# Retention projects v once and sums in four column tiles; RWKV mixes on VectorE; the order of the instructions chosen anew

## The reference

```python
xk = x * time_mix_k + shifted * (1.0 - time_mix_k)     # xv, xr alike
k = jnp.einsum('bsd,ed->bse', xk, Wk)                  # v from xv, r = sigmoid from xr
# per channel, a scan over the tokens: out = (e1*aa + e2*v) / (e1*bb + e2)
out = jnp.einsum('bsd,ed->bse', r * wkv, Wo)
```

```python
q = _rotate(split_heads(x @ Wq.T), cos, sin)           # k alike; v without rotation
retention = jnp.einsum('bhsd,bhtd->bhst', q, k) * SCALING * decay   # gamma_h ** (s - t)
out = jnp.einsum('bhst,bhtd->bhsd', retention, v)
out = (out - mean) * rsqrt(var + EPS) * gn_w + gn_b    # over the 8 of a head
return silu(x @ Wg.T) * out @ Wo.T
```

## Time and profile before

| | us |
|---|---|
| runs, median (lowest to highest of 3) | 724.55 (722.36 to 731.54) |
| the profiled execution, its own time | 730.31 |
| its span | 728.4 |
| PE busy | 606.1 (83%) |
| VectorE busy | 386.8 (53%) |
| ScalarE busy | 344.1 (47%) |
| GpSimd busy | 399.4 (55%) |
| PE weight loads busy | 513.3 (70%) |

### The profile page before, as it was taken

How to read it: one execution, slowest core, us unless ns; L and a number is a source line. 1 busy time by engine, 2 the same in 40 slices (tenths; PEclk the granted TensorE clock), 3 DMA queues, 4 the chain that set the end, 5 groups by cost and what they waited for, 6 DMA issues and landing times.

```text
span 728.4 us, 13112 instructions
## 1 busy us (share of the span) xinstructions
PE 606.1 (83%) x4180; PEld 513.3 (70%) x4180; DVE 386.8 (53%) x1056; ACT 344.1 (47%) x667; POOL 399.4 (55%) x400
## 2 busy tenths in 40 slices
PE   3398998999598886888789988999678989996891
PEld 2388977678576875878778878656644659886881
DVE  6513416797679753533162206797777985500005
ACT  2355556755367534653366567314233124653450
POOL 2556756674457645655556666632205764566662
PEclk9999999999699989997999999999969999999996
DMA  8345213112311223221142213100211111211314
GB/s 335 125 135 199 41 38 102 40 38 59 95 34 30 59 49 99 73 45 33 41 105 67 45 52 96 40 19 12 81 29 23 30 29 29 66 43 44 91 45 145
DMA packets 45121, 50.21 MB, mean 69 GB/s; under 512 B 14456, under 2 KB 36344, under 8 KB 45056
## 3 DMA queue, kind: packets, MB, share of 16 engines
q0 software_dynamic: 11776, 24.14, 13.5%
q1 hardware_dynamic: 31904, 24.44, 10.6%
q10 hardware_dynamic: 1376, 0.79, 0.4%
HBM read 32.04 MB, written 17.29 MB: 68 GB/s over the span
## 4 chain that ended last, share of the span: by engine, by line
PE 63%; DVE 10%; DMA 9%; issue 8%; ACT 5%; POOL 4%; ACTq 1%; POOLq 0%; DVEq 0%
PE bank L621 18%; PE bank L601 14%; PE bank L608 10%; DMA xs<-tokens_in,idx_in 6%; PE pair L709 5%; PE pair L741 3%; PE bank L582 2%; POOL xs L1101 2%; PE pair L545 2%; PE pair L525 2%; DMA tokens_out<-ys,idx_out 2%; POOL tokens_out L1113 1%; ACT w_up L840 1%; ACT hT L861 1%; ACT ys L908 1%
## 5 line engine op out<-in xcount | busy, mean ns | idle before, releaser
L1113 POOL DMA_INDIRECT tokens_out<-ys,idx_out x184 | 195.1, 1060 | 158.4 <-ACT ys L908 80.5
L1101 POOL DMA_INDIRECT xs<-tokens_in,idx_in x184 | 193.7, 1053 | 147.1 <-DVE owner L1261 36.6
L621 PE MATMUL bank<-w,hT 128*128 x1288 | 184.5, 288 | 22.7 <-ACT ys L908 10.4
L621 PEld LDWEIGHTS bank<-w,hT 128*128 128x128 f32 x1288 | 166.6, 199 | 41.1 <-issue 39.9
L601 PE MATMUL bank<-xT_kept,w_up 128*128 128x128 f32 x1104 | 163.2, 297 | 17.6 <-ACT gate L858 6.9
L601 PEld LDWEIGHTS bank<-xT_kept,w_up 128*128 128x128 f32 x1104 | 149.2, 209 | 31.8 <-issue 17.8
L840 ACT ACTIVATE w_up<-w 128x728 f32 (+1 forms) x184 | 128.9, 718 | 47.1 <-PE bank L608 17.3
L1281 DVE TENSOR_TENSOR hT<-gate,bank 128x384 f32<-128x384 f32 x92 | 50.5, 549 | 121.8 <-PE bank L601 60.8
L608 PE MATMUL bank<-xT_kept,w_up 128*128 128x128 f32 x736 | 101.6, 286 | 10.0 <-ACT hT L861 7.3
L608 PEld LDWEIGHTS bank<-xT_kept,w_up 128*128 128x128 f32 x736 | 92.4, 197 | 20.0 <-issue 11.9
L908 ACT ACTIVATE ys<-bank 128x256 f32<-128x256 f32 x96 | 35.9, 374 | 103.0 <-PE bank L621 52.6
(11 more groups left out here) (169 smaller groups left out, 639.6 us busy)
## 6 DMA issues: line engine op xcount, KB each, us to landing
yg<-tokens_out SPq DMA_DIRECT2D x60, 128.0 KB, 3.0
w<-in_w SPq DMA_DIRECT2D x8, 536.0 KB, 8.3
w<-in_w SPq DMA_DIRECT2D x8, 512.0 KB, 5.3
xs<-tokens_in,idx_in POOLq DMA_INDIRECT x184, 2.8
tokens_out<-ys,idx_out POOLq DMA_INDIRECT x184
tokens_in<-xn SPq DMA_DIRECT2D x8, 256.0 KB, 7.1
tokens_in<-xn SPq DMA_DIRECT2D x8, 254.0 KB, 2.5
sq<-in_square SPq DMA_DIRECT2D x1, 768.0 KB, 13.2
```

The lines of the kernel that those rows point to most:

```text
L621: last = mm(y, hT[0:n_f, n % 2, c * P:(c + 1) * P], w_of(k, e, WD[k] + c * P, P, n_f), start=(c == 0), stop=(k == 0 and c == CH[k] - 1))
L1101: pool.indirect_dma_start(xs[:, j % RING, :], None, xn_dram[KIND[f]][b], tile_rows(idx_in, b, j), engine_sem=described)\
L1113: pool.indirect_dma_start(ys_dram[b], tile_rows(idx_out, b, j), ys[:, j % RING, :], None, engine_sem=described)\
```

## The change

- **Retention, v.** v is projected once per batch (2 matmuls), its rows scaled by ScalarE into `zT`, stored to a new tensor in memory (`values0`, `values1`), and loaded eight times by SP (`values(b)`), each load giving all rows of a head its value j; 4 buffers of 1024 columns (`v_own`). VectorE multiplies k by such a buffer. The 8 rounds' products lie in 5 buffers, scanned in place; the order in VectorE's stream becomes scan n, key value n+1, query n.
- **Retention, sums.** After rounds 4 and 8, four matmuls with 32 output columns each (`tile_position=(0, 32*c)`) write the four quarters of the partitions. The weights of the mean are not there any more: v's weights are centred once on VectorE (`centred_values`). The accumulator is the batch's own PSUM pair. The rows of v, g, the norm's weights and Wo are in an order of 8 by 16.
- **RWKV.** `rwkv_weights` goes. VectorE makes the difference of x and shifted x and three blends (`rwkv_mixed`, new program steps before `rwkv_exponents`), and PE needs one matmul for each projection and half.
- **Others.** SP loads and stores all of the last results. `sq` is loaded in three parts. `TURNS` is new for every engine.

```diff
...
+QUAD = 32
+NQ = P // QUAD
+ROUNDS = DH // NQ
+J_AT = [n % NQ * ROUNDS + n // NQ for n in range(DH)]
+NVB = 4
+NMB = NQ + 1
...
     "pe":
-        "d a b3 e b9 e a2 e a2 d e a d a c d c e a2 c2 a d c a e a c d a c a2 c d a d e c a2 c d a4 d a d a c a e a3 d "
...
+        "d b e b11 e a2 e a e d a2 c d a c e a3 c d a c a c2 d c a4 c d c d c e a5 e d2 a d2 a2 c a3 d c a d a c a c a "
...
-        "a d a c a b c2 b c3 b c5 a6 b4 c b2 c a2 c a4 c b6 a4 b4 a2 b2 a3 d e d a b3 d b d e4",
+        "b a2 c a c2 b c5 b c3 a6 b5 c2 b d e a3 c a2 f a c b6 a4 f5 g f4 b4 a2 g9 b2 a2 d a2 d2 b4 d e4",
...
+            def values(b):
+                yield
+                sp.wait_ge(RE_ACT[b].sem, RE_ACT[b].done(0, "v1"))
+                sp.dma_start(v_dram[b], zT[:, b, :]).then_inc(st_v[b], 16)
+                by_head = v_dram[b].rearrange("(h j) t -> h j t", j=DH)
+                for n, j in enumerate(J_AT):
+                    yield
+                    if n == 0:
+                        sp.wait_ge(st_v[b], 16)
+                        if b == 0:
+                            sp.wait_ge(RS_PE.sem, RS_PE.done(0, f"rope{2 * NH - 1}"))
+                    if n >= NVB:
+                        sp.wait_ge(RE_DVE[b].sem, RE_DVE[b].done(0, f"kv{n - NVB}"))
+                    elif b:
+                        sp.wait_ge(RE_DVE[b - 1].sem, RE_DVE[b - 1].done(0, f"kv{DH - NVB + n}"))
+                    sp.dma_start(v_own[:, n % NVB, :], by_head[:, j, :].unsqueeze(1).to_broadcast([H, DH, S]))\
+                        .then_inc(ld_v[n % NVB], 16)
+
...
             def rwkv(b):
-                def project(name, i, j, to):
-                    mm(to[:], rw_w[:, 2 * j, :], xT_of(b, i * HALF, HALF), start=True, stop=False)
-                    yield
-                    mm(to[:], rw_w[:, 2 * j + 1, :], xnT[:, b, i * HALF:(i + 1) * HALF], start=False, stop=True)\
-                        .then_inc(RW_PE[b].sem, 1)
-
+                def project(i, j, mixed, to):
+                    mm(to[:], sq[:, M_MIX + j * P:M_MIX + (j + 1) * P], mixed[:, i * HALF:(i + 1) * HALF],
+                       start=True, stop=True).then_inc(RW_PE[b].sem, 1)
+
...
-                for j in range(DH):
-                    if j + 1 < DH:
-                        for i in range(NH):
-                            yield
-                            project(i, ret[:, T_V + (j + 1) * P:T_V + (j + 2) * P], i, (RE_DVE, f"kv{j + 1}"))
+                    if i == 0 and b == 0:
+                        after(RS_COPY, 0, "gate")
+                    project(i, ret[:, T_G:T_G + P], i, (RE_ACT, f"gate{i}"))
+                for r in range(ROUNDS):
                     for i in range(NH):
                         yield
-                        if j == 0 and i == 0:
-                            after(RT_DVE[1 - b], SUB[(3, 5)[b]], "out")
-                        after(RE_DVE[b], 0, f"m{j}")
-                        mm(bank[CB[1 - b] + i][:], ret[:, T_OUT + j * P:T_OUT + (j + 1) * P],
-                           r_m[:, j % 2, i * HALF:(i + 1) * HALF], start=(j == 0), stop=(j == DH - 1)).then_inc(RE_PE[b].sem, 1)
+                        if r == 0 and i == 0:
+                            after(RS_POOL, 0, "var")
+                            after(RS_BACK, 0, "back")
+                        after(RE_DVE[b], 0, f"m{r * NQ + NQ - 1}")
+                        to = take(CB[b] + i, RE_ACT[b], 0, f"sq{i}") if r == 0 else bank[CB[b] + i]
+                        for c in range(NQ):
+                            last = mm(to[c * QUAD:(c + 1) * QUAD, :], ret[:, T_OUT + r * QUAD:T_OUT + (r + 1) * QUAD],
+                                      r_m[:, (r * NQ + c) % NMB, i * HALF:(i + 1) * HALF], start=(r == 0),
+                                      stop=(r == ROUNDS - 1), tile_position=(0, c * QUAD))
+                        last.then_inc(RE_PE[b].sem, 1)
...
-                            after(RE_PE[b - 1], 0, "x1")
+                        act.wait_ge(ld_ret, 16 * 3)
+                    after(RE_PE[b], 0, f"v{i}")
+                    run(zT[:, b, parts[i]], bank[CB[b] + i][:], ACT.Copy, RE_ACT[b], scale=scale[:, 0:1])
...
+            def rwkv_mixed(b):
+                def step(ins):
+                    ins.then_inc(RW_MIX[b].sem, 1)
+
+                def blend(out, part, c):
+                    step(V.scalar_tensor_tensor(out[:, part], rw_t[:, part], colv[:, MIX + c:MIX + c + 1], xnT[:, b, part],
+                                                ALU.mult, ALU.add))
+
+                xk, xv, xr = rw_bb[:, 1:1 + S], rw_aa[:, 1:1 + S], zT[:, b, :]
+                for i in range(NH):
+                    part = slice(i * HALF, (i + 1) * HALF)
+                    yield
+                    after(NM_ACT[b], 1, f"xnT{i}")
+                    if i == 0:
+                        after(SETUP, 0, "sel")
+                        if b:
+                            after(RW_DVE[b - 1], 0, "num")
+                    step(V.tensor_tensor(rw_t[:, part], xT_of(b, i * HALF, HALF), xnT[:, b, part], ALU.subtract))
+                    after(RW_MIX[b], 0, f"d{i}")
+                    blend(xk, part, 0)
+                yield
+                blend(xv, slice(0, S), 1)
+                yield
+                blend(xr, slice(0, S), 2)
+
...
-                for j in range(DH):
-                    m = r_m[:, j % 2, :]
-                    yield
-                    after(RE_PE[b], 0, f"v{j}_{NH - 1}")
-                    done(f"S{j - 1}" if j else "k1")
-                    step(V.tensor_tensor(r_kv, k, pair[b], ALU.mult))
-                    yield
-                    done(f"kv{j}")
-                    step(V.tensor_tensor_scan(r_S, gamma[:, 0:1].to_broadcast([P, S]), r_kv, 0.0, ALU.mult, ALU.add))
-                    yield
-                    done(f"S{j}")
-                    if j >= 2:
-                        after(RE_PE[b], 0, f"o{j - 2}_{NH - 1}")
-                    step(V.tensor_tensor(m, q, r_S, ALU.mult))
+
+                def key_value(n):
+                    if n == 0:
+                        done("k1")
+                    if n >= NMB:
+                        after(RE_PE[b], 0, f"o0_{NH - 1}")
+                    dve.wait_ge(ld_v[n % NVB], 16 * (b * (DH // NVB) + n // NVB + 1))
+                    step(V.tensor_tensor(r_m[:, n % NMB, :], k, v_own[:, n % NVB, :], ALU.mult))
+
+                yield
+                key_value(0)
+                for n in range(DH):
+                    m = r_m[:, n % NMB, :]
+                    yield
+                    done(f"kv{n}")
+                    step(V.tensor_tensor_scan(m, gamma[:, 0:1].to_broadcast([P, S]), m, 0.0, ALU.mult, ALU.add))
+                    if n + 1 < DH:
+                        yield
+                        key_value(n + 1)
+                    yield
+                    done(f"S{n}")
+                    step(V.tensor_tensor(m, q, m, ALU.mult))
                 var, y, t = (r_st[:, a, :] for a in range(3))
...
+            def centred_values():
+                w = heads(sq[:, M_V:M_V + P], H, DH)
+                yield
+                dve.wait_ge(ld_sq, 16 * 3)
+                V.tensor_reduce(v_sum[:, :], w, AX.X, ALU.add).then_inc(RS_V.sem, 1)
+                after(RS_V, 0, "sum")
+                V.scalar_tensor_tensor(w, v_sum[:, :].unsqueeze(2).to_broadcast([P, H, DH]), -1.0 / DH, w, ALU.mult, ALU.add)\
+                    .then_inc(RS_V.sem, 1)
 
...
-            for pair in range(RING // 2):
-                act.wait_ge(st_ys[pair], 16 * (LAST + 1) * stored_from(pair))
-            act.wait_ge(ADD[1].sem, ADD[1].done(SUB[5] - 1, f"b{NT - 1}"))
-            for i in range(NT // 2):
-                load_result(act, 1, i, 1)
-            for t in range(3, NT, 4):
-                store_result(act, 1, t)
...
```

175 lines of the change are left out of this document (79 added, 96 removed), and 60 rows, old and new, of the table TURNS.

## The result

Over 20 runs of each, the changed kernel took 732.92 us (726.65 to 739.86) at the median and the kernel before 726.86 (722.36 to 731.83): a ratio of 1.0062 [1.0033, 1.0091], slower by 4.5 us (2.4 to 6.6) and within 2%. The ratio leaves out two of the changed kernel's runs, which fell in a slower state; by the two medians it is 6.1 us. The forecast was 719, a change of -5.7 us. Of the 14 us between 719 and 732.92, 2.3 lie in the kernel before, whose median was 724.55 over the three runs known then. The profiled execution took 730.91 us (span 729.1) beside 730.31 (span 728.4) before.

What follows compares the result with a forecast made beforehand. The prediction took mixers to be chains on VectorE, with PE filling the rest with experts and expert passes alone set by their pipeline. Its terms summed to -5.7 us, giving a forecast median of 719, range 690 to 735.

Steps and rivals of the forecast that it cites:

- new wait of 3.5 + 0.5 - 2.3 = 1.7 us a batch: Sixth key times value waits for the first sums group: +3.4 us for both batches (0 to +10.4).
- The load of PE: Rival: PE is the bound after all, most of its saved work is given back, 680 to 695 us; chance 0.22.
- v once: Retention: projecting v once per batch removes VectorE's waits for v between rounds, -4.6 us.
- First round: Start of retention's rounds: v's store and load hidden behind q and k; -1 us in batch 0, -2.5 in batch 1.
- v comes late: Rival: slow store and load delay the first rounds, +10 us on the forecast, 729 us; chance 0.12.
- the transfers pace the rounds: Rival: v's loads slower than 4.74 us set the rounds' pace, up to 776 us; chance 0.07.
- The tiles: Sums in column tiles: a group takes 1.8 to 7.0 us, 3.5 assumed, full overlap doubted because a matmul has two records.
- +1.7 a batch: Retention's tail: the last sums group stands before the variance, +3.4 us for both batches (0 to +10.4).
- RWKV's mixing: Mixing moved from PE to VectorE ahead of RWKV's first scan: +2.3 us batch 0, +0.5 batch 1, together +2.8.
- The start of retention: New order after pass (3,0): fewer gathers and up tiles ahead bring retention sooner, -1.5 us (0 to -5).
- The last stage: After the last routing table, 2.5 fewer expert tiles remain at 2.68 us a tile: -6.7 us.
- The end: Last results: SyncE issues all eight transfers instead of sharing them with ScalarE's queue, +2 us.

Runs made afterwards that it cites:

- 17: Changed kernel with GpSimd's first scatter of pass (5,0) behind 12 gathers instead of 10: 719.41 us against 725.92, 0.9916 of the kernel before.
- Number 6: Changed kernel with v's eight loads of batch 1 moving an eighth of their bytes: 0.9921 of the kernel before.
- 13: Kernel before, with v's projections for the second to the eighth round cut to 16 of 512 columns: 0.9966 of the kernel before.
- 14: Kernel before, with v's projections for rounds 2 to 8 and the sums of rounds 2 to 7 cut to 16 columns: 0.9942 of the kernel before.
- 7: Changed kernel with four extra 128-column matmuls on PE ahead of each down step of passes (3,1) and (5,0): 1.0369 of the kernel before.
- 11: Changed kernel with the sums' matmuls 128 output columns wide and without column tiles: 1.0136 of the kernel before.
- 5: The changed kernel, unedited, run again as a base on another chip: 0.9959 of the kernel before.
- 10: Changed kernel without RWKV's difference and blends, all three projections reading xnT: 0.9959 of the kernel before.
- 3: Changed kernel with the first sums group of batch 1 two steps earlier on PE: 0.9883 of the kernel before.
- 16: Changed kernel with six product buffers and the first sums group of batch 1 two steps earlier on PE: 1.0021 of the kernel before.
- 12: Changed kernel with batch 1's tail steps two tiles sooner on PE and ScalarE, first gathers of (5,1) four scatters sooner: 0.9979 of the kernel before.
- 4: Changed kernel with six gathers of pass (3,1) back ahead of the last two scatters of (3,0) on GpSimd: 1.0029 of the kernel before.
- 2: Changed kernel with three of four down matmuls per tile left out in the last pass: 0.9914 of the kernel before.
- 1: Changed kernel with GpSimd waiting before each indirect transfer instead of every second: 1.0281 of the kernel before.
- 8: Changed kernel with GpSimd waiting only before every fourth indirect transfer: 1.0547 of the kernel before.
- 15: Changed kernel with eight extra small matmuls ahead of four groups of transposes of pass (5,0): 1.0062 of the kernel before.

## Why the prediction was wrong, point by point

**The step that failed: "With half a microsecond for expert work ahead on PE that is a new wait of 3.5 + 0.5 - 2.3 = 1.7 us a batch".** In batch 0 it was 1.94, in batch 1 9.81: 8.1 us more than forecast in one wait, where the kernel lost 4.5 in all. The group itself was shorter than I took it (1.92 us, 2.92 at half clock); the work ahead of it on PE was not half a microsecond but two tiles' steps that waited for gathers, 7.3 us in two waits. I priced the queue on PE by its own work and did not ask what the step ahead waits for, two engines back, although the order of turns shows a scatter between the tenth and the eleventh gather. The tail of batch 1 was mis-sized too, see below. The run that shows the first is 17: with only that scatter moved, the wait fell from 9.81 to 0.62, the rounds from 46.0 to 36.7 us (551.31 to 588.01), and table (5,1) came 5.2 us sooner behind its predecessor; of the other 4 us, 1.2 stand ahead of the first round and 2.8 behind the variance (VectorE waited 6.7 us at the gates, 3.9 in the changed kernel), and the wait of 9.86 for the variance itself stayed. The time went to 0.9 of a per cent below the kernel before. Against the changed kernel it was not timed in one job; the quotient of the ratios is 0.985, 10.6 us, but the changed kernel's own ratio differed by 1% between two chips, so the size is uncertain by as much. The two profiles differ by 6.1 us from table (3,1) on.

Transfers issued at that place are dear: in the rounds of batch 1 an indirect transfer took 1.6 us on GpSimd, 1.0 elsewhere; so it did before, but with two gathers late (3.0 us of PE's time), not five (13.9). Number 6 says that it is not the bytes of v's loads alone: an eighth of them left 1.4 to 2.9 us, though the gap fell by 4.0 us. The Trainium skill's page "SBUF — State Buffer", section "Who interferes with whom", says that a VectorE instruction with two inputs in SBUF contends with a GpSimd instruction that reads SBUF; the same section infers that such an instruction did not hold up the making of descriptors, which needs the write interface. Key times value became one with this change, its v came from PSUM before, and batch 0's transfers went from 1.34 us to 1.65; but batch 1's did not get dearer (1.62 before, 1.54 now). No run isolated what makes them dear.

**"The load of PE" as a rival (0.22).** Refuted for the kernel before, and the forecast's own reading with it confirmed: 13 and 14 took 24 and 44 us of PE work out of it by their estimate, without a change of order, and gave 2.5 and 4.2 us by their ratios; the two retention stages kept their 144 and 89 us. A stretch that shows 67.0 of 67.0 us busy was not limited by PE. Yet PE's time is not slack either: 7 added 35 us of busy time to the changed kernel, and 4.1% of the time, some 32 us, was lost. Each insertion stands ahead of steps that others wait for; that this is the reason was not tested. So taking work out won next to nothing and putting work in cost nearly all of it.

**v once, "-4.6".** Those waits did go; in their place stood the new ones. 13 does not price them: 3.6 of the 4.6 us stayed there, for the light projections stood in the same queue on PE, behind late gathers. What I had not foreseen: a round became 4.46 us (467.07 to 471.53) where it was 4.83 (559.82 and the next at 564.65) or, at the least, 4.72. No instruction of a round stands directly behind the one that it needs any more, since the next key times value and the last query product stand between: some 0.3 us a round, 5 us in all. The earlier trace rows gave 4.74 and the order of the change showed the interleaving.

**First round, "-1" and "-2.5".** In batch 0 the forecast was right about the cover: from 449.76, PE's first projection, to 461.30 are 11.5 us with no wait for a load (13.4 before); nothing between the loads and VectorE ever waited. In batch 1 the 3.34 us for v went, 2.4 us for q and k came behind the table, and two of the twelve steps of the rotation that stood ahead of the table before stood behind it: +0.3. The rivals *v comes late* and *the transfers pace the rounds* fell with it: loads landed in 7.0 us at the median, above the 5.3 of the earlier trace rows, and four ahead was enough.

**The tiles.** Overlap is full: 1.92 us against 7.09 in 11, 3.7 times, and 11 lost 1.8%, about 14 us, against 5 on another chip and against 10 in its own job (1.0136, and 0.9959 both). The low end of the range (1.8) was right; my doubt about a second record behind the first was not. The Trainium skill's page "TensorE: Matmul & The Clock Gate", Part 3, has 2.38 for three tiles; four gave 3.7 here. No row shows a price of the change of mode: the next matmul starts at 484.51, before the 1.92 us from 482.65 are over. In the tail, +1.7 a batch was +0.1 and +4.1: in batch 1 an up step at half clock (3.6 us) and a wait for ScalarE stood ahead, and 3 and 16 show that a first group that comes sooner only makes that tail longer (21.8 and 18.2 us). 12, which moved the tail's steps two tiles up, had 7.8 us for the variance where 5 had 11.6, and paid for it behind the table.

**RWKV's mixing, "+2.8".** VectorE's first scan of batch 0 started 7.4 us behind the first copy to xnT (125.52 to 132.90), 4.7 before (127.50 to 132.15): +2.7 where +2.3 was said. Whether the program pays for it is open: 10, without the mixing, had the same ratio as 5, but an effect of 2.8 us is smaller than its interval, and its table (2,0), 202.2 us, lies within the 199.2 to 204.6 of kernels that mix. The +3.0 of the table is within what same code shows.

**The start of retention, "-1.5 (0 to -5)".** The last scatter of (3,0) went from 432.60 to 426.11, the first round by -5.0. 4 put the gathers back: the scatter 6.7 us later, the stage 5.1 longer, the whole 0.7% slower than 5, in another job on the same chip. The low bound was the value.

**The last stage, "-6.7".** The windows of line 649 alone, as the earlier trace rows:

```profile
639.00:714.00 75.00, 30.02 (x200) 27.12 (x200) 0.93 0.24 62
```

200 records are in this window, and the last tile's eight start at 714.10, just behind it: 208, where the kernel before has 224 (225 in the two windows of the earlier trace rows, one counted twice). That is two tiles fewer, 2.5 were forecast, and no time was won. A tile's share of that stretch (2.68 us) is not its price, since GpSimd takes part in the pace: behind the last table it issues one indirect transfer each 1.6 us (0.97 busy, then 0.30 or 0.75 idle in turn, and a few longer waits), 50 transfers where there were 51. No single bound explains it: 18 us less PE work (2) gave 0.45% of the whole and 5.7 us of the stage against 5, in another job; one more wait per transfer (1) cost 3.2%; fewer waits (8) cost 5.9%. 12 shows the exchange: 8.9 us won ahead of the table, 7.7 given back behind it.

**The end, "+2".** From the last scatter's end to the end of the span were 11.5 us, 11.8 before: SyncE's eight issues cost nothing.

**The clock.** The span's mean granted clock was 0.901, 0.940 before. Around the late sums it was at its lower level, 1.2 GHz: the down tile at 577.11, behind two waits of 5.89 and 1.36 us, took 2.07 us, where the one at 480.61 took 1.06, and the group 2.92 instead of 1.92. That is 2 of the 9.81. Within the 20 runs the time was longer where the clock was lower (correlation -0.86), which does not say which is the cause; 15 raised it a little in the stage that lost, and won nothing. In 14 the granted clock between tables (3,1) and (5,1) was 0.87, 0.95 before, and these stages were no longer (233.5 and 234.2 us). I can't say what part of the 4.5 us it is.

**What would show it.** Share 78% (77 said), rounds with one gap, the first scan after xnT: right. First round after 11.5 us: a little sooner than the 12 to 14 said. Table (5,1) at +1.2 us (-2 said) and the last pass unmoved: wrong. The tables between 190 and 428 us moved by up to 5.8 ((2,0), from 185.79 to 191.57), one of them over the 5 that I gave.

## What to carry to other kernels

A new wait is as long as everything ahead of the work that it waits for: follow that queue back through each engine until a row has no releaser, the indirect transfers above all. Removing an engine's work without moving anything is the cheap test of whether it is a bound; a window that is 100% busy need not be one, and work put back can still cost its full time. In a pipeline with a hand-written order, one scatter ahead of two gathers can outweigh 39 us of saved TensorE time.

## What the runs showed of the hardware

- Four column tiles of 32 with float32 data of 512 columns: 16 records in 1.92 us at full clock, 2.92 (579.21) at lower, against 7.09 for 16 of 128 output columns one behind the other.
- On VectorE, another instruction between each of the two dependent pairs of a round (128x1024, float32) saved some 0.3 us a round: 4.46 instead of 4.72 to 4.83.
- Indirect transfers cost GpSimd 0.97 us each and 1.6 with its waits in the last stage, and 1.54 and 1.65 us each at the mean, up to 2.9, beside retention's rounds. GpSimd shows 55% busy over the span, and one more wait per transfer (1) cost 3.2%. Four between waits instead of two (8) made the whole 5.5% slower than the kernel before.
- The same code had ratios of 0.9959 [0.9918, 1.0000] and 1.0062 [1.0033, 1.0091] on two chips: a difference of 1% between two versions needs one job.
